# A decoder layer on one core: GpSimd makes a slot's scan inputs as one product and normalises the attention, which ScalarE copies out of PSUM

## The reference

```python
x = x + attention(layernorm(x))           # 4 sequences of 512, 16 heads of 32, 2 kv heads, causal
x = x + mamba(ctx_1024, z=layernorm(x))   # the middle term below
x = x + moe(layernorm(x))                 # 16 experts, 2 for each token, and a shared expert

# attention, per head:
scores = Q @ K.T / sqrt(32); scores = where(causal, -inf, scores)
out = softmax(scores) @ V                 # then out @ Wo + bo

# mamba, 512 channels, 16 states n, time t:
state = state * exp(dt * A[:, n]) + (dt * u) * B[n, t]
y[t] = sum over n of state[n, t] * C[n, t]
y = (y + D * u) * silu(z)
```

## Time and profile before

| what | value |
|---|---|
| median of 3 runs | 1224.88 us (1223.96 to 1228.74) |
| profiled execution | 1226.14 us |
| its span | 1224.3 us |
| middle stage | 171.4 to 703.4 us of the span |
| engines over the span | PE 88%, DVE 66%, POOL 55%, ACT 55% |

### The profile page before, as it was taken

The page is one execution under the profiler, slowest core; times in us unless marked ns, Lnnn a source line. Parts: engine busy times, 40 slices in busy tenths (PEclk is TensorE's granted clock), DMA queues, the critical chain, the costliest instruction groups (busy, mean ns, idle before and its releaser), DMA issues. The chain is left out here.

```text
span 1224.3 us, 18632 instructions
## 1 busy us (share of the span) xinstructions
PE 1080.4 (88%) x6368; PEld 646.6 (53%) x6368; DVE 809.5 (66%) x1199; ACT 668.2 (55%) x1438; POOL 673.5 (55%) x587
## 2 busy tenths in 40 slices
PE   7999838888888888888888799999999989999994
PEld 3444416555555555555555544544444456667651
DVE  5477769999999999999999657740681023333328
ACT  3566768988888898888888622411010112222220
POOL 1033368999999999999999560201031224444420
PEclk9999959999999999999999999999999989999997
DMA  6210000111011111111232031212205534334229
GB/s 206 88 36 19 18 18 27 35 36 32 30 36 36 35 28 35 37 32 56 86 104 70 1 139 47 91 45 93 69 0 191 174 118 132 125 130 128 70 63 375
DMA packets 51932, 94.74 MB, mean 77 GB/s; under 512 B 9918, under 2 KB 18110, under 8 KB 51840
## 3 DMA queue, kind: packets, MB, share of 16 engines
q1 hardware_dynamic: 44320, 72.82, 18.3%
q0 software_dynamic: 7520, 20.72, 5.5%
HBM read 74.51 MB, written 20.84 MB: 78 GB/s over the span
## 5 line engine op out<-in xcount | busy, mean ns | idle before, releaser
L604 POOL TENSOR_TENSOR w_all<-w_all 128x512 f32<-128x512 f32 x256 | 321.2, 1275 | 1.5 <-DVE w_all L778 1.2
L778 DVE TENSOR_TENSOR_SCAN w_all<-da,w_all 128x512 f32<-128x512 f32 x256 | 297.7, 1204 | 0.0
L712 ACT ACTIVATE da<-w_all,a_flat 128x512 f32<-128x512 f32 x256 | 179.4, 701 | 9.0 <-PEq L96 7.7
L683 PE MATMUL yb<-ident,w_all 128*128 128x128 f32 x1024 | 163.0, 282 | 7.2 <-DVE acc L786 7.2
L633 PE MATMUL sc<-w_all,attn 32*128 32x384 f32 (+3 forms) x512 | 106.2, 492 | 44.3 <-ACT w_all L720 21.7
L720 ACT ACTIVATE w_all<-sc,neg_max 128x128 f32<-128x128 f32 (+3 forms) x256 | 134.1, 540 | 17.5 <-DVE neg_max L770 16.5
L659 PE MATMUL ob<-w_all,v 128*32 128x128 f32 x1280 | 95.7, 280 | 52.6 <-ACT w_all L729 52.6
L683 PEld LDWEIGHTS yb<-ident,w_all 128*128 128x128 f32 x1024 | 114.6, 142 | 36.9 <-issue 30.8
L770 DVE TENSOR_REDUCE neg_max<-sc 128x2 f32<-128x256 f32 (+3 forms) x128 | 104.1, 813 | 35.6 <-PE sc L636 35.6
L1189 POOL TENSOR_TENSOR w_all<-w_all 128x512 f32<-128x512 f32 x24 | 29.4, 1226 | 165.0 <-ACT w_all L1360 165.0
L729 ACT ACTIVATE w_all<-tb 128x256 f32<-128x256 f32 (+2 forms) x192 | 102.7, 535 | 30.8 <-PE tb L648 30.8
(11 more groups left out here) (193 smaller groups left out, 1638.8 us busy)
## 6 DMA issues: line engine op xcount, KB each, us to landing
w_all<-b_scratch SPq DMA_DIRECT2D x64, 256.0 KB, 3.3
w_all<-in_w_up SPq DMA_DIRECT2D x16, 512.0 KB
w_all<-in_w_down SPq DMA_DIRECT2D x16, 512.0 KB
w_all<-sorted_y SPq DMA_DIRECT2D x16, 512.0 KB, 11.2
attn<-in_x SPq DMA_DIRECT2D x4, 1024.0 KB, 6.8
w_all<-in_x SPq DMA_DIRECT2D x16, 256.0 KB, 4.1
norms<-attn SPq DMA_DIRECT2D x4, 1024.0 KB, 4.3
out_dram<-acc SPq DMA_DIRECT2D x16, 256.0 KB, 8.8
```

The costliest lines, as they stand in the source:

```text
L604: pool.tensor_tensor(dbu[:, k, :], keep["du"][i // N][:, k * T:(k + 1) * T], b_all[i % 2][:, :], ALU.mult).then_inc(pool_dbu.sem, pool_dbu ...
L683: last = pe.transpose(yb[which][:, k * P:(k + 1) * P], state[i % 2][:, k, t * P:(t + 1) * P], ident[:, :])
L712: act.activation(da[unit % 2][:, :], keep["dt"][i // N][:, k * T:(k + 1) * T], ACT.Exp, scale=keep["a_flat"][:, unit % (N * KD):unit % (N ...
L778: dve.tensor_tensor_scan(state[i % 2][:, k, :], da[unit % 2][:, :], dbu[:, k, :], 0.0, ALU.mult, ALU.add).then_inc(dve_scan.sem, dve_scan. ...
```

## The change

- GpSimd's `weigh` makes two of the four slots of `dbu` in one instruction (128x1024, B's row repeated), once a step. It waits until both slots were scanned. VectorE waits for it in front of every second scan; SP's waits are counted in pairs.
- ScalarE copies `ob` to `attn` as it is (`copy_out`), behind the copy of the reciprocals. TensorE's next use of `ob` waits for this copy.
- GpSimd multiplies `attn` by `r_all` in place (`normalize`), in the step after, behind the product and ahead of the addition. VectorE's `normalize` is gone. The loop of GpSimd has one step more.
- In `experts` the four saved blocks count on one semaphore, and every wait is for all four.

```diff
         @block.sync
-                    sp.wait_ge(pool_dbu.sem, pool_dbu.upto(3 * N * KD - 1))
+                    sp.wait_ge(pool_dbu.sem, pool_dbu.upto(3 * N * KD // 2 - 1))
...
-                sp.wait_ge(pool_dbu.sem, pool_dbu.upto(4 * (i - 2) + 3))
+                sp.wait_ge(pool_dbu.sem, pool_dbu.upto(2 * (i - 2) + 1))
...
         @block.gpsimd
-            def weigh(unit):
-                i, k = unit // KD, unit % KD
+            def weigh(pair):
+                i, k = pair // 2, 2 * (pair % 2)
                 if k == 0:
                     pool.wait_ge(s_b_all[i % 2].sem, s_b_all[i % 2].upto(i // 2))
-                if unit >= 4:
-                    pool.wait_ge(dve_scan.sem, dve_scan.upto(unit - 4))
-                pool.tensor_tensor(dbu[:, k, :], keep["du"][i // N][:, k * T:(k + 1) * T], b_all[i % 2][:, :], ALU.mult).then_inc(pool_dbu.sem, pool_dbu.tick(unit))
+                if pair >= 2:
+                    pool.wait_ge(dve_scan.sem, dve_scan.upto(2 * pair - 3))
+                pool.tensor_tensor(dbu[:, k:k + 2, :], keep["du"][i // N].rearrange("p (k t) -> p k t", k=KD)[:, k:k + 2, :],
+                                   b_all[i % 2].rearrange("p (a t) -> p a t", a=1).broadcast_to([P, 2, T]), ALU.mult).then_inc(pool_dbu.sem, pool_dbu.tick(pair))
...
+            def normalize(quad):
+                b, m = quad // NT, quad % NT
+                out = keep["attn"][:, b, m * T:(m + 1) * T]
+                pool.wait_ge(act_turn.sem, act_turn.upto(turn["r", quad]))
+                pool.wait_ge(act_out.sem, act_out.upto(quad))
+                pool.tensor_tensor(out, out, r_all[:, :], ALU.mult).then_inc(pool_norm.sem, pool_norm.tick(quad))
+
             weigh(0)
-            weigh(1)
-            for g in range(UNITS + 3):
+            for g in range(UNITS + 4):
                 if g + 1 < UNITS:
-                    weigh(2 * g + 2)
+                    weigh(g + 1)
+                if spread_in(g - 1) is not None:
+                    normalize(spread_in(g - 1))
                 if 0 <= g - 3 < UNITS:
                     add(g - 3)
-                if g + 1 < UNITS:
-                    weigh(2 * g + 3)
...
         @block.tensor
                 if unit % 8 == 0 and unit >= 8:
-                    pe.wait_ge(dve_out.sem, dve_out.upto(unit // 8 - 1))
+                    pe.wait_ge(act_out.sem, act_out.upto(unit // 8 - 1))
...
         @block.scalar
             def spread(quad):
                 act.wait_ge(pe_turn.sem, pe_turn.upto(turn["r", quad]))
                 if quad >= 1:
-                    act.wait_ge(dve_out.sem, dve_out.upto(quad - 1))
+                    act.wait_ge(pool_norm.sem, pool_norm.upto(quad - 1))
...
+            def copy_out(quad):
+                b, m = quad // NT, quad % NT
+                act.wait_ge(pe_pv.sem, pe_pv.upto(8 * quad + 7))
+                act.activation(keep["attn"][:, b, m * T:(m + 1) * T], ob[:, :], ACT.Copy).then_inc(act_out.sem, act_out.tick(quad))
...
                 if spread_in(g) is not None:
                     spread(spread_in(g))
+                    copy_out(spread_in(g))
...
         @block.vector
-                dve.wait_ge(pool_dbu.sem, pool_dbu.upto(unit))
+                if unit % 2 == 0:
+                    dve.wait_ge(pool_dbu.sem, pool_dbu.upto(unit // 2))
...
-            def normalize(quad):
-                b, m = quad // NT, quad % NT
-                dve.wait_ge(pe_pv.sem, pe_pv.upto(8 * quad + 7))
-                dve.wait_ge(act_turn.sem, act_turn.upto(turn["r", quad]))
-                dve.tensor_tensor(keep["attn"][:, b, m * T:(m + 1) * T], ob[:, :], r_all[:, :], ALU.mult).then_inc(dve_out.sem, dve_out.tick(quad))
...
-                if spread_in(g) is not None:
-                    normalize(spread_in(g))
...
         # experts
-        s_keep = [signal(f"keep{b}", 16) for b in range(B)]
+        s_keep = signal("keep", 16)
...
-            for b in range(1, B):
-                sp.wait_ge(s_keep[b].sem, s_keep[b].upto(0))
+            sp.wait_ge(s_keep.sem, s_keep.upto(B - 1))
...
-            for b in range(B):
-                pool.wait_ge(s_keep[b].sem, s_keep[b].upto(0))
+            pool.wait_ge(s_keep.sem, s_keep.upto(B - 1))
...
-            for b in (0, LAST):
-                act.wait_ge(s_keep[b].sem, s_keep[b].upto(0))
+            act.wait_ge(s_keep.sem, s_keep.upto(B - 1))
```

More of the change, by code:

```diff
@@ L546, in mix @@
         pe_s, pe_turn, pe_y, pe_pv = [signal("pe_" + n) for n in ("s", "turn", "y", "pv")]
-        act_da, act_p, act_turn, act_cy = [signal("act_" + n) for n in ("da", "p", "turn", "cy")]
-        dve_max, dve_scan, dve_acc, dve_rinv, dve_out = [signal("dve_" + n) for n in ("max", "scan", "acc", "rinv", "out")]
-        pool_dbu, pool_acc = [signal("pool_" + n) for n in ("dbu", "acc")]
+        act_da, act_p, act_turn, act_cy, act_out = [signal("act_" + n) for n in ("da", "p", "turn", "cy", "out")]
+        dve_max, dve_scan, dve_acc, dve_rinv = [signal("dve_" + n) for n in ("max", "scan", "acc", "rinv")]
+        pool_dbu, pool_acc, pool_norm = [signal("pool_" + n) for n in ("dbu", "acc", "norm")]
         s_b_all = keep["s_b_all"]
@@ L1134, in save @@
                 sp.wait_ge(dve_n.sem, dve_n.upto(4 * b + 3))
-                sp.dma_start(d["norms"][b, :, :].rearrange("(t p) c -> p t c", p=P), z[b]).then_inc(s_keep[b].sem, s_keep[b].tick(0))
+                sp.dma_start(d["norms"][b, :, :].rearrange("(t p) c -> p t c", p=P), z[b]).then_inc(s_keep.sem, s_keep.tick(b))
             def expert(e):
```

## The result

| | before | changed |
|---|---|---|
| median | 1225.0 us (22 runs) | 1227.37 us (22 runs) |
| profiled execution, its span | 1226.14, 1224.3 us | 1226.73, 1225.0 us |

The ratio is 1.0017, 95% interval 1.0009 to 1.0025: 2.1 us slower (1.1 to 3.1), a small loss, but one that stands clear of the scatter of the runs. The forecast was +1.7 us, 1226.6 us.

What follows compares the result with a forecast made beforehand. TensorE's queue, which releases the four-tile row maximum, was taken to bound the middle stage's chain, not VectorE. Start +0.68 and end +1.03 summed to +1.7 us, the other terms 0: 1226.6 us, range 1220 to 1236.

Steps and rivals of the forecast that it cites:

- VectorE's 25.6 us are worth 0: Middle stage: losing 11.1 us of normalisation and 14.5 us of waiting gains 0, as TensorE's scores release the row maximum.
- ScalarE's copy just fits: ScalarE's queue before the four-tile exponent: the added copy needs 0.49 us of 0.51 us room, so costs 0.
- GpSimd: Middle stage: a pair product takes 2.46 us, 30.8 of 32.58 us a quad; cost 0, bound only above 2.69 a pair.
- the list of signs: Expected trace marks: VectorE idle before L770 some 57 us, quad 32.58, pair 2.4 to 2.5, stage end 1.7 us later.
- GpSimd's added work slows nobody: VectorE's scans beside GpSimd's added normalisation: the scan's mean stays; were it not so, 20 us more.
- The start: Start of the middle stage: the first pair product delays the first scan, so the second row maximum comes 0.68 us later.
- The end: End of the middle stage: ScalarE's copy, then GpSimd's 1.28 us product, end near 704.1, not 703.07; +1.03 us.
- The single semaphore: Last stage: one semaphore for the four saved blocks costs 0, either way at most some tenths.
- VectorE's wait before the maximum: VectorE's idle time before the row maximum (L770), by TensorE: up from 35.6 to some 57 us.
- the first rival: Middle stage: VectorE was the bound after all; all 25.6 us back gives 1201 us, work only 1215.5; 12 in 100.

Runs made afterwards that it cites:

- the second normalisation: VectorE's normalisation made twice, the first into a scratch tile, on the kernel before: 1227.07 us, ratio 1.0026.
- the second copy: ScalarE's copy of `ob` made twice, the first into a scratch tile, on the changed kernel: 1236.92 us, ratio 1.0099 to the kernel before.
- the profile with single products: The changed kernel with GpSimd's products made one by one again, with the old handshake: 1226.45 us, ratio 1.0015 to the kernel before.
- the ends mended: The changed kernel with GpSimd's first two products made one by one and VectorE normalising the last quad out of PSUM: 1223.6 us, ratio 0.9995 to before.
- the move on the kernel before: The kernel before with TensorE's spread of the reciprocals moved behind the next scores, VectorE normalising after the four-tile maximum: 1236.14 us, ratio 1.0094.

## Why the prediction was right

- *VectorE's 25.6 us are worth 0*: right, with its mechanism. The wait for the scores grew in the step by what had gone (0.44 to 1.81), and the second normalisation cost 0.07 us a quad.
- *ScalarE's copy just fits*: right, with 0.05 us to spare where 0.02 were worked out. The exponent comes 1.26 us behind the maximum before and after; the second copy shows 0.42 of its 0.47 us a quad. With so thin a cover, that it held is in part luck: a copy 0.05 us longer would have begun to show.
- *GpSimd*: a pair took 2359 ns, a start-to-start distance of 2.31 us, against 2.46 forecast (2.4 to 2.5 in the list of signs) and 2.69 where it would have decided. GpSimd is off the chain up to 32.0 us of work a quad, and on it at 34.5. The estimate of 2.25 us from the Trainium skill's "GPSIMD Engine Reference", section "Elementwise — side-by-side cycle accounting", was 0.11 us under the record.
- *GpSimd's added work slows nobody*: right, the scan's mean is 1206 ns beside the 1204 of before, and 1208 with four more products a quad, where GpSimd is never idle; so the trace agrees with "SBUF — State Buffer", section "Who interferes with whom", in the Trainium skill.
- *The start*: +0.68 forecast, +0.63 in the first steps. That all of it is kept was right: it is still 0.62 at the ninth maximum, against the profile with single products whose clock rose in the same step (32.62 and 33.24 us after the first product). Only against the profile of the kernel before is it hidden, by the clock.
- *The end*: +1.03 forecast, +1.12 measured. GpSimd began its product 0.14 us after the copy had ended, where 0.06 was assumed. That is 0.08 of the 0.09.
- *The single semaphore*: 0 forecast; with the ends mended the ratio is 0.9995 (0.9983 to 1.0008) with it in. A few tenths of a microsecond either way would not show.

The sum of the two ends by their timelines, 1.75 us, lies inside the measured 1.1 to 3.1 us.

Details that missed: VectorE's wait before the maximum came to 55.4 us, not 57. The forecast added 1.37 us for all 16 normalisations, but behind the last one stands no maximum: its wait of 4.36 us in the earlier trace rows was the drain of the stage. 35.6 + 15 x 1.37 is 56.2, and 0.8 us of other waits for the scores went too. For the same reason the 25.6 us that "all came back" in the first rival were never all to be had. The quads and ends of the two doubled operations explain only 1.7 of 3.2 and 7.6 of about 10 us, and that of the four added products came out 2 to 3 us under its forecast.

## What to carry to other kernels

Work taken off the busiest engine pays only if the next instruction is not waiting for another engine anyway: look at the instruction after the one that goes, and at who releases it. Compare a step that has the work with one that hasn't; here the 0.94 us between the two half-quads came from TensorE's spread, in another queue than the normalisation. A copy that frees a buffer early may be worth nothing until the order that the buffer dictated is changed too.

## What the runs showed of the hardware

TensorE's granted clock fell from 2.4 to 1.2 GHz for about 3.4 us in the middle of the stage only in kernels whose TensorE waits more: three times in the move on the kernel before (near 282.6, 548.8 and 682.0), once with ScalarE's copy doubled, and five times with GpSimd as the bound (once for some 10 us). One of them, in the move on the kernel before:

```profile
682.00:685.00 3.00, 3.00 (x16) 2.47 (x13) 2.62 (x3) 0.84 (x4) 1.27 (x1) 0.50 0.02 5
```

A quad with such a fall took 0.8 to 1.2 us more (33.83 for 33.00, 34.23 and 34.27 for 33.07), so a cost in waits may draw a second one behind it. That rests on one profile of each kernel, and what in TensorE's work sets the fall off was not tried.

GpSimd's records were longer where its queue never ran empty: with four more products a quad the pair took 2462 ns by its record, and 2359 to 2362 in the other kernels with pairs. The starts of neighbouring instructions stayed 2.31 and 1.23 us apart. So a queue's room is worked out from the distances of the starts and not from the records.
